# Two normalised 3x3 convolutions on one core: GpSimd takes the input's low part of every second chunk of the first image, and the serial chain ahead of the first convolution is rewritten

## The reference

```python
x = x + _L0_conv_ref(_gn(x), w_fft_real, w_fft_imag, rot_w, rot_b, bn_gamma, bn_beta)
x = x + _L1_conv_ref(_gn(x), L1_conv_weight)
```

```python
angle = jnp.tanh(angle) * (jnp.pi / 4)
cos_theta = jnp.cos(angle)[:, 0]
phase = jnp.exp(-2j * jnp.pi * (cos_theta[:, None, None, None] * fsum))   # fsum: sums of three frequencies in {0, 1/3, -1/3}
rotated = jnp.fft.ifftn(w_fft[None] * phase[:, None, None], axes=(-3, -2, -1)).real
w2d = rotated[:, :, :, 1, :, :]          # the middle slice: 3x3 taps of this image
```

## Time and profile before

| | us |
|---|---|
| median of 3 runs | 1844.71 |
| the profiled execution, its own time | 1844.59 |
| its span in the profile | 1842.8 |
| PE busy | 1667.6 (90%) |
| DVE busy | 1430.5 (78%) |
| ACT busy | 1136.3 (62%) |
| POOL busy | 123.6 (7%) |

### The profile page before, as it was taken

The page is one execution under the profiler, slowest core; times in us unless marked ns, Lnnn a source line. Parts: engine busy times, 40 slices in busy tenths (PEclk is TensorE's granted clock), DMA queues, the critical chain, the costliest instruction groups (busy, mean ns, idle before and its releaser), DMA issues.

```text
span 1842.8 us, 65260 instructions
## 1 busy us (share of the span) xinstructions
PE 1667.6 (90%) x29275; PEld 1428.3 (78%) x29275; DVE 1430.5 (78%) x2222; ACT 1136.3 (62%) x944; POOL 123.6 (7%) x357
## 2 busy tenths in 40 slices
PE   6878888367669999999999999999999999999899
PEld 5777888233346667998899799979997999799755
DVE  6989999579987878888788878787878887787500
ACT  6887888235546665666566566656665666566444
POOL 0000000110020002001000200020002000100100
PEclk9999999789989999999999999999999999999999
DMA  9999999144446655666566656556665666566245
GB/s 386 421 421 422 421 422 422 69 126 132 120 121 205 202 198 183 210 204 197 187 203 200 202 182 213 198 181 211 204 199 184 205 206 200 182 204 199 105 181 203
DMA packets 101974, 411.57 MB, mean 223 GB/s; under 512 B 17139, under 2 KB 19688, under 8 KB 85352
## 3 DMA queue, kind: packets, MB, share of 16 engines
q1 hardware_dynamic: 101064, 407.88, 63.0%
q0 software_dynamic: 672, 0.08, 0.1%
HBM read 271.82 MB, written 136.07 MB: 221 GB/s over the span
## 4 chain that ended last, share of the span: by engine, by line
PE 65%; DVE 19%; DMA 6%; issue 5%; POOL 3%; ACT 1%; SPq 1%; DVEq 0%; POOLq 0%; ACTq 0%
PE ps L385 33%; PE ps L378 30%; DVE x L599 6%; DMA x<-x_pix 5%; DVE stats L866 3%; DVE nat L818 3%; DVE x L831 3%; POOL x L526 1%; ACT x L454 1%; POOL sm L571 1%; PE ps L329 0%; POOL sm L570 0%; POOL x L529 0%; PE ps L330 0%; DVE stats L899 0%
## 5 line engine op out<-in xcount | busy, mean ns | idle before, releaser
L378 PE MATMUL ps<-nat,wc 64*64 64x512 f16 (+1 forms) x12480 | 1271.9, 382 | 73.2 <-DVE nat L818 40.8
L385 PE MATMUL ps<-x,wc 64*64 64x512 f16 (+1 forms) x12585 | 1253.2, 376 | 12.8 <-POOL x L579 12.2
L378 PEld LDWEIGHTS ps<-nat,wc 64*64 64x64 f16 x12480 | 726.7, 108 | 196.2 <-issue 49.2
L385 PEld LDWEIGHTS ps<-x,wc 64*64 64x64 f16 x12585 | 734.3, 107 | 105.2 <-POOL x L579 15.7
L476 ACT ACTIVATE nat<-xin,gnp 128x1024 f16<-128x1024 f32 (+1 forms) x264 | 299.8, 1137 | 352.5 <-PE ps L378 336.7
L486 ACT ACTIVATE x<-ps,gnp 128x1024 f16<-128x1024 f32 (+1 forms) x264 | 289.7, 1097 | 184.2 <-DVE stats L866 184.1
L831 DVE SCALAR_TENSOR_TENSOR x<-ps,gnp,x 128x1024 f16<-128x1024 f32 (+1 forms) x264 | 333.1, 1262 | 6.1 <-ACT x L486 5.9
L497 ACT ACTIVATE outb<-ps,bias 128x1024 f32<-128x1024 f32 (+1 forms) x264 | 289.6, 1097 | 77.4 <-PE ps L385 62.5
L866 DVE BATCH_NORM_STATS2 stats<-ps 128x6 f32<-128x512 f32 (+1 forms) x520 | 335.7, 686 | 0.1
L818 DVE SCALAR_TENSOR_TENSOR nat<-xin,gnp,nat 128x1024 f16<-128x1024 f32 (+1 forms) x264 | 331.3, 1256 | 0.3 <-ACT nat L476 0.3
L329 PE MATMUL ps<-x 128*128 128x129 f16 x2048 | 259.0, 227 | 58.5 <-DVE x L599 58.3
(11 more groups left out here) (134 smaller groups left out, 212.1 us busy)
## 6 DMA issues: line engine op xcount, KB each, us to landing
x<-x_pix SPq DMA_DIRECT2D x128, 1024.0 KB, 13.6
xin<-x_tiles SPq DMA_DIRECT2D x256, 512.0 KB, 3.8
out<-outb SPq DMA_DIRECT2D x256, 512.0 KB, 4.1
xin<-x_tiles SPq DMA_DIRECT2D x8, 192.5 KB, 2.4
out<-outb SPq DMA_DIRECT2D x8, 192.5 KB, 2.9
w<-taps_scratch SPq DMA_DIRECT2D x64, 8.0 KB, 1.9
w<-taps_scratch SPq DMA_DIRECT2D x32, 16.0 KB, 2.6
taps_scratch<-x POOLq DMA_DIRECT2D x21, 3.0 KB, 2.0
```

The lines of the kernel that those rows point to most:

```text
L378: return nc.tensor.matmul(ps[64 * kind:64 * kind + 64, bank, 0:w], lhs, nat[rows, xhl, a:a + w], start=first, stop=last)
L385: ins = nc.tensor.matmul(ps[64 * kind:64 * kind + 64, bank, done:done + part], lhs, x1[rows, xhl, z:z + part], start=first and done == 0, ...
```

## The change

Two things are changed.

**GpSimd makes some low parts.** Chunks 5, 7, ..., 31 of the first image (14 of them, `on_pool`) get their low part on GpSimd in two passes: a `tensor_scalar` that scales `xin` in place, and a `tensor_tensor` that subtracts the high part. VectorE's `lo0(g)` does nothing for these; its `lo0(g+1)` first waits for GpSimd's `pool_lo` and counts `lo0_ready` up on its behalf.

**The opening chain is rewritten.** Instructions that don't depend on each other are issued without a wait between them (`go` and `need` beside `link`), three-part loops become one instruction on a broadcast operand, scale factors move into constants, and each of the three angles' sines comes straight from ScalarE's Sin with a scale and a bias for each row. `Z_TAPS` is 48 in place of 82. The padding of the first four chunks is done by VectorE while TensorE makes the taps, ScalarE no longer waits for `Z_S` ahead of `hi0`, the four first low parts come ahead of `weights0`, and of the 12 loads of the first weights SP's queue issues 8 and GpSimd's the other 4, ahead of its 21 `taps_out`.

```diff
+        w_soft = sem("w_soft")
+        pool_lo = sem("pool_lo")
...
+        def on_pool(g):
+            return NX < g < NFULL and g % 2 == 1
...
             taps_out(sp, 0, zdma)
             hold(sp, zdma, 16 * 4)
-            load_weights(0)
+            load_weights(sp, 0, ((1, 0), (1, 1)), w_in)
...
-            nc.scalar.activation(zc[:, 232:240], zc[:, 224:232], ACT.Tanh).then_inc(zac, 1)
-            act.wait_ge(zve, Z_COSARG)
-            nc.scalar.activation(zc[:, 248:256], zc[:, 240:248], ACT.Sin).then_inc(zac, 1)
-            act.wait_ge(zve, Z_PHASE)
-            nc.scalar.activation(zc[:, 272:288], zc[:, 256:272], ACT.Sin).then_inc(zac, 1)
+            nc.scalar.activation(zc[:, 232:240], zc[:, 224:232], ACT.Tanh, bias=zc[:, 188:189]).then_inc(zac, 1)
+            act.wait_ge(zac, 3)
+            nc.scalar.activation(zc[:, 248:256], zc[:, 232:240], ACT.Sin, bias=c("quarter"), scale=math.pi / 4
+                                 ).then_inc(zac, 1)
+            act.wait_ge(zac, 4)
+            trig = c("trig", 2 * K3)
+            for k in range(2):
+                nc.scalar.activation(zc[0:2 * K3, 256 + 8 * k:264 + 8 * k], zc[0:2 * K3, 248:256], ACT.Sin,
+                                     bias=trig[:, 2 * k + 1:2 * k + 2], scale=trig[:, 2 * k:2 * k + 1]).then_inc(zac, 1)
...
-            act.wait_ge(zve, Z_S)
             for g in range(NX):
                 hi0(g)
...
             pool.wait_ge(zve, Z_TAPS)
-            pool.wait_ge(zdma, 16)
+            pool.wait_ge(zdma, 16 * 4)
+            load_weights(pool, 0, ((0, 0), (0, 1)), w_soft)
             for b in range(1, B):
                 taps_out(pool, b, taps_rest)
+            def low_part(g):
+                a = (g % NX) * CH
+                pool.wait_ge(hi0_ready, g + 1)
+                link(G.tensor_scalar(xin[:, g % NX, :], xin[:, g % NX, :], gnp[:, 1, 0:1], 1.0, ALU.mult, ALU.mult))
+                G.tensor_tensor(nat[:, 1, a:a + CH], xin[:, g % NX, :], nat[:, 0, a:a + CH], ALU.subtract
+                                ).then_inc(pool_lo, 1)
             for b in range(B):
                 rows = 0
-                for n in (7, 15, 23, NFULL - 1, NFULL):
+                for n in range(NCH):
+                    if b == 0 and on_pool(n + NX):
+                        low_part(n + NX)
+                    if n not in (7, 15, 23, NFULL - 1, NFULL):
+                        continue
...
             def lo0(g):
+                if on_pool(g):
+                    return
+                if on_pool(g - 1):
+                    ve.wait_ge(pool_lo, (g - NX) // 2)
+                    ve.sem_inc(lo0_ready, 1)
                 ve.wait_ge(hi0_ready, g + 1)
...
+            def go(ins):
+                count[0] += 1
+                ins.then_inc(zve, 1)
+                return count[0]
+            def need(step):
+                ve.wait_ge(zve, step)
+            def link(ins):
+                need(go(ins))
+                return count[0]
...
-            link(V.tensor_scalar(gram, gram, 1.0 / (AS * AS * NPIX), None, ALU.mult))
...
-            for k in range(3):
-                n = link(V.tensor_scalar(wa[:, :, k], inv, rw[:, k:k + 1], None, ALU.mult))
-            at(n, Z_WA)
+            at(link(V.tensor_tensor(wa, by_form(inv), rw[:, :].unsqueeze(1).to_broadcast([C, B, 3]), ALU.mult)), Z_WA)
...
-            link(V.tensor_tensor(s2, s1, c1, ALU.mult))
...
-            link(V.scalar_tensor_tensor(sf, s3[0:n2, :], smk[:, 2:3], sf, ALU.mult, ALU.add))
...
+            after_act(3)
+            go(V.tensor_tensor(ztb, by_image(cf), by_tap(c("u", n2)), ALU.mult))
+            after_act()
+            link(V.tensor_tensor(zub, by_image(sf), by_tap(c("v", n2)), ALU.mult))
+            at(link(V.tensor_tensor(ztb, ztb, zub, ALU.add)), Z_T)
+            for g in range(NX):
+                pad(g)
+            after_pe()
+            at(link(V.tensor_copy(tapsb, ps[0:9 * B, 6, 0:256])), Z_TAPS)
...
             def weights0(b, part):
                 if part == 0:
-                    ve.wait_ge(w_in, 16 * 12 * (b + 1))
+                    ve.wait_ge(w_in, 16 * (12 * b + 8))
+                    if b == 0:
+                        ve.wait_ge(w_soft, 16 * 4)
...
             for g in range(NX):
-                pad(g)
+                lo0(g)
             for part in range(4):
                 weights0(0, part)
-            for g in range(NX):
-                lo0(g)
             pad(NX)
```

More of the change, by code:

```diff
@@ L1 @@
+import math
 from contextlib import ExitStack
@@ L63 @@
 _FIRST = [("mask_g", 128), ("fold", 16), ("rep", 128), ("pair", 16), ("id16", 16),
-          ("ones", 128), ("u", 9), ("v", 9), ("cm", 4), ("sm", 3), ("image", 8)]
+          ("ones", 128), ("u", 9), ("v", 9), ("trig", 4), ("quarter", 1), ("image", 8)]
 def places(table):
@@ L217, in taps_out, with load_weights @@
                               ).then_inc(signal, 16)
+        def load_weights(eng, b, groups, signal):
+            for half, r in groups:
+                for ci in range(2):
+                    g = ((half * 2 + r) * 2 + ci) * C
+                    for rows, m in (((r, 4), 0),) if half == 0 else (((2 + r, 2), 0), ((r, 2), 128)):
+                        eng.dma_start(w32[g:g + C, m:m + 64 * rows[1]].rearrange("c (a m) -> c a m", m=64),
+                                      taps[b, :, rows[0]:rows[0] + rows[1], ci:ci + 4, :].rearrange(
+                                          "c a q o -> c a (q o)")).then_inc(signal, 16)
         def reads(n):
@@ L632, in at @@
[L632 to L643, removed]
@@ L653, in _ @@
[L653 to L659, removed]
@@ L684, in _ @@
[L684 to L714, removed]
-            at(link(V.tensor_scalar(bv, bv, 1.0 / B, BN_EPS, ALU.mult, ALU.add)), Z_BNVAR)
@@ new lines, in after_act, with at @@
+            def after_act(times=1):
+                act_steps[0] += times
+                ve.wait_ge(zac, act_steps[0])
+            def at(k, n):
+                assert k == n, (k, n)
+            link(V.memset(zpad, 0.0))
+            ve.wait_ge(a_mask, B + 2)
+            at(link(V.tensor_scalar(colsum, colsum, AS, None, ALU.mult)), Z_SUMS)
+            after_pe()
+            for hh in range(2):
+                n = go(V.tensor_reduce(gram[:, 4 * hh:4 * hh + 4, :],
+                                       ps[0:C, 2 + hh, :].rearrange("p (b k c) -> p b c k", b=4, k=8),
+                                       AX.X, ALU.add))
@@ new lines, in _ @@
+            go(V.tensor_copy(zc[0:C, 0:8], ps[0:C, 4, 0:8]))
+            need(n)
+            diag = wtmp[0:C, 0:B * C].rearrange("p (b c) -> p b c", b=B)
+            link(V.tensor_tensor(diag, gram, c("id16", C).unsqueeze(1).to_broadcast([C, B, C]), ALU.mult))
+            at(link(V.tensor_reduce(zc[0:C, 8:16], diag, AX.X, ALU.add)), Z_MOM)
+            after_pe()
+            gmean, scale0, self0, conv0 = (zc[0:C, 320 + 8 * k:328 + 8 * k] for k in range(4))
+            both, roots, tmp2, invs = zc[0:C, 32:48], zc[0:C, 48:64], zc[0:C, 304:320], zc[0:C, 16:32]
@@ new lines, in _, with by_image, by_tap @@
+            link(V.tensor_tensor(bo(qs), bo(qs), by_b(bi), ALU.mult))
+            at(link(V.tensor_reduce(zc[:, 224:232], bo(qs), AX.X, ALU.add)), Z_ANGLE)
+            n2 = 2 * K3
+            cf, sf = zc[0:n2, 256:264], zc[0:n2, 264:272]
+            ztb, zub = (a.rearrange("p (b t) -> p b t", t=9) for a in (zt, zu))
+            def by_image(a):
+                return a.unsqueeze(2).to_broadcast([n2, B, 9])
+            def by_tap(a):
+                return a.unsqueeze(1).to_broadcast([n2, B, 9])
@@ L996 @@
 Z_SUMS = 2
-Z_MOM = Z_SUMS + 4 + 2
-Z_VAR = Z_MOM + 5
-Z_WA = Z_VAR + 5 + 4 + 3
-Z_FORMS = Z_WA + 1 + 6 + 1
-Z_BNVAR = Z_FORMS + 2 + 2 + 3 + 2 + 3 + 2 + 2
-Z_ANGLE = Z_BNVAR + 5 + 1 + 3 + 1
-Z_COSARG = Z_ANGLE + 1
-Z_PHASE = Z_COSARG + 2
-Z_T = Z_PHASE + 10 + 6 + 3
+Z_MOM = Z_SUMS + 5
+Z_VAR = Z_MOM + 4
+Z_WA = Z_VAR + 4 + 1
+Z_FORMS = Z_WA + 3 + 4 + 1
+Z_BNVAR = Z_FORMS + 3 + 10
+Z_ANGLE = Z_BNVAR + 4 + 3
+Z_T = Z_ANGLE + 3
 Z_TAPS = Z_T + 1
```

191 lines of the change are left out of this document (85 added, 106 removed).

## The result

The changed kernel takes 1839.7 us (median of 11 runs, 1837.2 to 1843.1) against 1844.4 for the kernel before beside it: a ratio of 0.9975 (95% interval 0.9966 to 0.9984), 4.7 us less. Forecast were 1833.5 us and 11 us less. The direction was right, but the gain is less than half. The time lies outside the forecast's own range of 1830 to 1837 us, and inside the wider one of 1829.5 to 1842.

The account below looks back on a forecast made before the run. The chain mask, statistics, `hi1`, `lo1` was taken to set the step, with a serial opening ahead of it. 1844.6 - 13.4 (opening) + 2.5 (offload) gave 1833.5 to 1834 us; own range 1830 to 1837, wider 1829.5 to 1842.

Parts of the forecast that it names:

- the reading of the step: First image's steps: `lo1` waits for `hi1` anyway, so VectorE's 14 saved low parts gain 0 (bound 17.8 us).
- the opening: Everything up to the first matmul of the convolutions: 9.2 us saved up to the taps plus 4.2 after, 13.4 us.
- the trigonometry: Opening, Tanh to `Z_T`: 6.92 us become 2.85 with three Sins at 0.2 to 0.25 each, 4.1 us saved.
- rival (d): The opening gives less, GpSimd's four weight loads landing 2 to 4 us late: 1836 to 1838 us; chance 0.10.
- the passes: GpSimd's two passes for each offloaded low part: 3.4 us together, in a round of 7.9 that just fits two steps.
- (a): Rival: GpSimd's passes take 3.9 to 4.3 us, costing 7 to 13 us, so 1838 to 1844; chance 0.16.
- (b): Rival: GpSimd's round bounds the first image, slower than before; 1859 us with passes of 5.4; chance 0.07.
- 2.9 us for this stretch: In GpSimd's round, TensorE's time from a low part's end to the mask, read from 510.03 to 512.93.
- most pads slip by: Padding copies after each mask mostly miss GpSimd's passes, some held up to 1 us; 2.5 us on all, bounds 0 and 14.

Follow-up runs that it names:

- e6: The changed kernel, but GpSimd counts `lo0_ready` itself and ScalarE writes the padding of chunks 5 to 31; 1830.6 us.
- e12: e6 with only chunks 5, 9, ..., 29 on GpSimd, `lo1` still in its own step; 1830.3 us.
- e8: e6 with only chunks 5, 9, ..., 29 on GpSimd and `lo1` made one step late; 1824.2 us.
- e1: The changed kernel with no chunk given to GpSimd, so the rewritten opening alone; 1829.9 us.
- e7: The changed kernel with TensorE running 10 pairs of constant matmuls before waiting for each of GpSimd's 14 chunks; 1835.5 us.

## Why the prediction was wrong, point by point

**Right: the reading of the step.** That `lo1` waits for `hi1` until the same moment, so that 17.8 us of VectorE's work are worth nothing. The earlier trace rows had it, e6 and e12 show it, and e8, which differs from e12 in that wait alone, turns it into a gain.

**Right: the opening.** 13.4 us worked out, 13.2 to the first matmul in the trace, 14.9 between the medians with e1. In its parts the trigonometry gave 3.8 of 4.1: ScalarE's activations with a column for scale or bias take 0.30 us for 128 rows and 0.38 for 54, not 0.2. The weights were never late, and GpSimd's four loads took 0.58 us each for 0.61. That rival (d) falls.

**Right in size: the passes**, 3.25 us for 3.4, so the rivals (a) and (b), slower passes, fall with their mechanism. The time came out in (a)'s stretch of 1838 to 1844 for other reasons.

Its 2.9 us for this stretch, from the earlier trace rows, is the right number by luck. The row shows the mask of chunk 31, where TensorE runs at a granted clock of 0.50 after an idle of 3.73 us. Its matmuls in the timeline, and the busy line of one microsecond of them:

```profile
510.08 5.33 PE L378 MATMUL ps<-nat,wc 64*64 64x512 f16 x48 [3.73 <-DVE nat L818]
```

```profile
511.00:512.00 1.00, 1.00 (x16) 0.49 (x12) 0.31 (x1) 0.00 (x0) 0.00 (x0) 0.50 0.92 156
```

The mask comes at 512.93, about half-way through these 48 matmuls; the masks of the changed kernel need all 48 (2.79 us at full clock), and half of them at half speed take about as long as all at full speed. The row that was taken for TensorE's normal pace already held the fallen clock.

**Mis-sized: the padding copies.** That "most pads slip by" gave 2.5 us for all that the offload costs; the pads alone are 4.6 us in the trace and 5.7 in the runs. The mechanism had its row and its place was named, but the passes' times were taken as fixed to the mask, while a late mask, a wrap copy or partial statistics shifts them onto the next pad each time: nine pads were held. The low clock is part of it, for a later TensorE makes a later pass (in e7 six are held and for less). `weights0`, too, has instructions with two inputs in SBUF, and two of them met a pass; no term stood for that.

Together the offload cost 9.8 us for 2.5, and the opening gave 14.9 for 13.4: -11 became -4.7 (-5.1 by these two).

## What to carry to other kernels

Work taken from an engine is worth only what the next wait leaves: look for a step in the trace that lacks the instruction already, as the earlier trace rows did.
